# Last row chunk of the last round loaded one strip wide instead of the last two; ScalarE makes most of the last scalings

## The reference

```python
# layer 0: e is x times two small weights
h   = adj @ (adj.T @ e)
out = layernorm(h) * gamma + beta + x
x   = layernorm(x + out)
# layer 1
deg  = adj.sum(axis=0) + 1.0
dinv = rsqrt(deg)
z    = dinv[:, None] * (x @ W)
out  = dinv[:, None] * (adj.T @ z + z) + b
x    = layernorm(x + relu(out))
```

## Time and profile before

| | us |
|---|---|
| median of three runs | 608.97 |
| the profiled execution's own time | 609.2 |
| its span in the trace | 607.4 |
| TensorE matmul busy | 578.3 (95%) |
| VectorE busy | 346.3 (57%) |
| ScalarE busy | 178.5 (29%) |
| GpSimd busy | 115.2 (19%) |

### The profile page before, as it was taken

The page is one execution under the profiler, slowest core; times in us unless marked ns, Lnnn a source line. Parts: engine busy times, 40 slices in busy tenths (PEclk is TensorE's granted clock), DMA queues, the critical chain, the costliest instruction groups (busy, mean ns, idle before and its releaser), DMA issues.

```text
span 607.4 us, 10911 instructions
## 1 busy us (share of the span) xinstructions
PE 578.3 (95%) x4648; PEld 219.9 (36%) x4648; DVE 346.3 (57%) x464; ACT 178.5 (29%) x432; POOL 115.2 (19%) x166
## 2 busy tenths in 40 slices
PE   9979999999999999999999999999999999877794
PEld 6423333333333333333333334544433334222232
DVE  3996676878868676986766694555520004400026
ACT  2035080633618062351807148334000001000001
POOL 3007052250706132050504114101000000000000
PEclk9989999999999999999999999999999999999998
DMA  9999796969788795978889597799999999999992
GB/s 312 386 377 363 249 350 223 389 221 354 269 307 319 260 386 190 384 270 307 287 287 387 187 391 271 293 399 378 422 421 422 421 419 422 420 420 423 412 387 101
DMA packets 77401, 204.82 MB, mean 337 GB/s; under 512 B 4126, under 2 KB 6686, under 8 KB 68136
## 3 DMA queue, kind: packets, MB, share of 16 engines
q1 hardware_dynamic: 76288, 203.27, 88.6%
q10 hardware_dynamic: 1064, 0.84, 0.4%
HBM read 202.79 MB, written 1.31 MB: 336 GB/s over the span
## 4 chain that ended last, share of the span: by engine, by line
PE 79%; DMA 14%; SPq 3%; DVE 2%; ACT 1%; issue 0%; DVEq 0%
PE psum L876 32%; PE psum L969 24%; PE psum L1056 14%; DMA turned<-in_adj_dram 7%; PE psum L977 5%; DMA slot<-in_adj_dram 4%; SPq L308 3%; DMA last_slot<-in_adj_dram 3%; PE psum L1076 1%; PE psum L931 1%; PE psum L1034 1%; PE psum L943 1%; SPq L312 0%; DVE slot L699 0%; DVE C L751 0%
## 5 line engine op out<-in xcount | busy, mean ns | idle before, releaser
L693 DVE STREAM_TRANSPOSE slot<-slot 128x2048 f32<-128x2048 f32 x80 | 178.1, 2281 | 68.4 <-PE psum L876 68.4
L876 PE MATMUL psum<-slot,E 128*64 128x512 f32 x800 | 180.0, 597 | 1.2 <-DMA slot<-in_adj_dram 0.7
L969 PE MATMUL psum<-slot,T 32*64 32x512 f32 x2560 | 144.1, 596 | 3.3 <-DVE T L674 3.3
L1056 PE MATMUL psum<-slot,E 128*64 128x512 f32 x480 | 106.2, 594 | 11.2 <-DMA slot<-in_adj_dram 11.0
L876 PEld LDWEIGHTS psum<-slot,E 128*64 128x64 f32 x800 | 54.4, 137 | 113.0 <-issue 108.8
L422 POOL COPY turned<-last_slot 32x1024 f32<-32x1024 f32 x80 | 84.1, 1052 | 38.9 <-issue 31.2
L969 PEld LDWEIGHTS psum<-slot,T 32*64 32x64 f32 x2560 | 55.9, 133 | 89.5 <-issue 82.1
L483 ACT ACTIVATE turned<-last_slot 32x1024 f32<-32x1024 f32 x80 | 84.3, 1054 | 5.3 <-DVE last_slot L693 3.6
L817 DVE TENSOR_TENSOR T<-psum,dinv 128x256 f32<-128x256 f32 x10 | 4.2, 424 | 134.5 <-PE psum L1076 134.0
L1056 PEld LDWEIGHTS psum<-slot,E 128*64 128x64 f32 x480 | 35.2, 137 | 79.1 <-issue 78.9
L475 ACT ACTIVATE T<-turn 32x186 f32<-32x186 f32 (+4 forms) x200 | 53.5, 309 | 21.2 <-DVE turn L668 19.0
(11 more groups left out here) (112 smaller groups left out, 273.1 us busy)
## 6 DMA issues: line engine op xcount, KB each, us to landing
slot<-in_adj_dram SPq DMA_DIRECT2D x152, 1024.0 KB, 14.2
last_slot<-in_adj_dram SPq DMA_DIRECT2D x30, 1024.0 KB, 7.8
turned<-in_adj_dram SPq DMA_DIRECT2D x9, 1024.0 KB, 16.1
X<-in_x_dram SPq DMA_DIRECT2D x5, 256.0 KB, 4.4
turned<-in_adj_dram SPq DMA_DIRECT2D x2, 512.0 KB, 12.1
out_dram<-T ACTq DMA_DIRECT2D x6, 128.0 KB, 7.0
out_dram<-T SPq DMA_DIRECT2D x4, 128.0 KB, 2.6
beta_b<-in_L_gnn_ln_beta_dram SPq DMA_DIRECT2D x1, 32.0 KB, 11.6
```

What stands on the lines that cost most here:

```text
L693: v.transpose(parts, parts).then_inc(chunk_cut, 1)
L876: return mm(acc[half[b % 2], :], E[:, b, :], view[:, b % CB, :], start=(b < 2), stop=(b >= NB - 2))
L969: last = mm(acc[half[h], a, :], T[step % 2][rows_a, jb, d, :], slot[step % 2][rows_a, h:NF:2, :, cols], start=step == 0 and jb == 0 and d ...
L1056: last = mm(bank[ACC[RES + n // NB * WIDE + s]][half[b % 2], :], E[:, b, :], wide[i % PLACES][:, s * JW:(s + 1) * JW], start=(b < 2), stop ...
```

## The change

`TAIL` becomes 76: loads 72 to 75 are wide, with chunk 8's four row blocks for all four strips, and only chunk 9 is loaded one strip at a time, by loads 76 to 79 (strips 6, 7, 8, 9). A strip turns complete with each of these loads. `turn_o(6)` comes after the sweep of load 77, `turn_o(7)` after that of 78, `turn_o(8)` and `turn_o(9)` after that of 79.

In strips 6, 7 and 8 ScalarE makes all four scalings, in strip 9 the first two. For that VectorE makes `shift = -mean * rstd` (one operation of 128x4, kept in `rsum`, two places), and ScalarE computes `rstd * o + shift` with an Identity activation whose scale and bias are columns in SBUF. `o` and `rstd` have two places in turn, so that strip J waits for the scalings of strip J - 2 only. This holds for all ten strips.

```diff
-TAIL = LOADS - WIDE * 2
+TAIL = LOADS - WIDE
+SCALED = {NJ - 4: 4, NJ - 3: 4, NJ - 2: 4, NJ - 1: 2}
...
+        shift = rsum[:, :].rearrange("p (i b) -> p i b", b=JB)
...
         def tail_part(n):
-            i = n - TAIL
-            return NQ - 2 + i % 2, NJ - WIDE + i // 2
+            return NQ - 1, NJ - WIDE + n - TAIL
...
-                    before_tail = 2 * (NJ - 1 - J) if J >= NJ - WIDE else 0
+                    before_tail = NJ - 1 - J if J >= NJ - WIDE else 0
...
                 nc.scalar.activation(std[:, 0:JB], mean_var[:, :, 1], ACT.Sqrt, bias=eps_col[:, 0:1])\
                   .then_inc(o_root, 1)
+                blocks = SCALED.get(J, 0)
+                if blocks:
+                    act.wait_ge(o_shift, J - NJ + WIDE + 1)
+                    if J >= RES:
+                        act.wait_ge(out_stored[J % RES], J // RES * 16)
+                for jb in range(blocks):
+                    nc.scalar.activation(Y[1][:, J % RES * JB + jb, :], Y[0][:, J % 2 * JB + jb, :], ACT.Identity,
+                                         bias=shift[:, J % 2, jb:jb + 1], scale=rstd[:, J % 2 * JB + jb:J % 2 * JB + jb + 1])\
+                      .then_inc(out_ready, 1)
...
-                o, r = Y[0][:, 0:JB, :], rstd[:, 0:JB]
+                lo = J % 2 * JB
+                o, r = Y[0][:, lo:lo + JB, :], rstd[:, lo:lo + JB]
...
-                if J >= 1:
-                    dve.wait_ge(out_ready, JB * J)
+                if J >= 2:
+                    dve.wait_ge(out_ready, JB * (J - 1))
...
-                for jb in range(JB):
+                ours = SCALED.get(J, 0)
+                if ours:
+                    v.scalar_tensor_tensor(shift[:, J % 2, :], mean_var[:, :, 0], -1.0, r, ALU.mult, ALU.mult)\
+                     .then_inc(o_shift, 1)
+                for jb in range(ours, JB):
...
             for n in range(TAIL, LOADS):
                 tail_sweep(n)
-                if n % 2 == 0 and n > TAIL:
-                    turn_o(NJ - WIDE + (n - TAIL) // 2 - 1)
+                if n > TAIL:
+                    turn_o(NJ - WIDE + n - TAIL - 1)
             turn_o(NJ - 1)
```

More of the change, by code:

```diff
@@ L226, in build @@
         o_root = sem("o_root")
+        o_shift = sem("o_shift")
         out_ready = sem("out_ready")
```

## The result

The changed kernel was slower: 612.23 us median of 13 runs (611.46 to 614.98) against 609.92 of 13 (607.56 to 610.84), ratio 1.0051 with a 95% interval of 1.0035 to 1.0067. The medians are 2.3 us apart, the ratio says 3.1. Four more timings of the same kernel gave 1.0032 (1.0011 to 1.0052), 1.0012 (0.9994 to 1.0030), 1.0043 (1.0024 to 1.0062) and 1.0040 (1.0021 to 1.0058). The mean of the five is 1.0036, 2.2 us. The first was the highest of them. Two executions of all that follow, one of 689.8 us and one of 1550.1, were disturbed and are in no ratio.

A forecast was written before the change was run, and what follows sets the result against it. DMA bounds the kernel from 540 us, VectorE already sets the end by 0.4 us. Loads 0.9 us sooner, but strips queuing on VectorE, give +2.10 us: 609.2 to 611.3, median 0.2 lower, 611.1; range 609.3 to 612.8.

The forecast's parts named there:

- The loads: Loads 72 to 75 at the end of the stream: made wide, they bring all that follows 0.9 us sooner.
- TensorE and the start of strip 6: TensorE's sweeps and turnings at the end: VectorE starts strip 6 at 593.71 us, before at 586.37.
- The queue: Strips 6 to 9 at the end: they queue on VectorE from 593.71 us, one every 3.20 us instead of 4.07.
- The next strip starts at 3.20: VectorE in the last strips: the shift ends 3.16 us after a strip's start, the next strip starts at 3.20.
- the two are level, and I count no wait: Start of strip 8: ScalarE's path takes 6.39 us from strip 6's start, VectorE's two periods 6.40, so no wait.
- ScalarE's scaling: One scaling on ScalarE takes 0.45 us at a pace of 0.35, four take 1.50.
- Rival (b): ScalarE's scalings hold up the copies of strips 8 and 9; 612.5 us at 0.60 each; chance 0.14.
- The split of strip 9's scalings: Last strip, scalings shared by ScalarE and VectorE: ends 4.00 us after its start, against 3.96 with all four on VectorE.
- The sum: End of the kernel: the last scaling moves from 605.21 to 607.31 us, +2.10 us, store and end unchanged.
- About 0.5%, 3 us, is what a measurement of this kernel tells from no change.: Whole kernel's timing: smaller differences count as no change, which got 0.75.
- TensorE's work is no more than it was.: TensorE at the end, sweeps and turnings up to sweep 79's end at 598.4 us: no work added.

The follow-up runs named there:

- Chunk 8 narrow: The changed kernel, but loads 72 to 75 bring chunk 8 one strip at a time; ratio 1.0064 to the kernel before.
- The tail alone: The kernel before with only the change's new load order (TAIL = 76), one place and all scalings on VectorE; ratio 1.0080 to the kernel before.
- scalings twice: The changed kernel with four more ScalarE activations before the scalings of strip 6 and four before those of strip 7; ratio 1.0064 to the kernel before.
- the version that beat both: The changed kernel, but loads 72 to 75 bring chunks 8 and 9 for strips 6 and 7 only; ratios 0.9970 and 0.9981 to the kernel before.

## Why the prediction was right or wrong

The time, 612.23 us, lies within the range, 1.1 above the 611.1 that was said. Of this 0.95 is the kernel before, which took 609.92 in this timing and not 608.97. The direction failed: 0.75 was given to no change that can be told, and the kernel was slower, 1.0051 with an interval clear of 1. Two steps failed; they stand behind those that held.

**The loads.** Right. Said: 0.9 us sooner. Chunk 8 narrow puts it at 0.88 where strip 6 starts and at 0.8 at the end.

**TensorE and the start of strip 6.** Right. Said: 593.71, 18.35 behind the pair; measured 594.49 - 576.21 = 18.28.

**The queue.** The mechanism was right: four strips on VectorE with no time between them, one in 3.2 us where the loads bring one in 2.7. The tail alone shows its cost, 4.7 us; the scalings on ScalarE and the two places take back 2.9 of it, where 2.4 were said. Two sizes were off. "The next strip starts at 3.20": the next strip begins 0.08 after the shift begins, while the shift still runs (597.46, 597.54), so the period is 3.05. And "the two are level, and I count no wait" holds for strip 9 but for strip 8 the path over ScalarE came 0.17 later than VectorE. Strips 6 to 9 took 9.34 instead of 9.60.

**ScalarE's scaling.** Worked out from rows as 0.45 at a pace of 0.35, four in 1.50; measured 0.426 and four in 1.44. The Trainium skill's formula ("ScalarE: Activation LUTs", section "What ACT_TABLE_LOAD costs") gave 0.425 and 1.42, so the trace agrees with the page better than with my rows. Rival (b) was closer to deciding than its 0.14 says: scalings twice shows that four more activations, 1.33 us on ScalarE, are paid in full, and the root behind them as well. The split of strip 9's scalings was said to take 4.00 us for the strip against 3.96 with VectorE alone; it took 3.93 (603.83 to 607.76).

**The sum.** Said: +2.10 for the place of the change; the profile has +1.75 (and 33.8 us from the pair instead of 34.1). The 0.35 less are 0.07 at the start of strip 6, 0.26 in the queue, 0.07 in strip 9, and 0.05 more behind it. Put against the timings, the sum was good: +2.10 is 0.35%, and the mean of the five ratios says 0.36%. Part of that is luck, since a sum 0.35 too high stood in for what the timings have above the place.

**"About 0.5%, 3 us, is what a measurement of this kernel tells from no change."** This step failed, and it turned a right sum into a wrong call. The sum says 0.35% slower, and this sentence made no change of it, with 0.75. No row stood behind it. The interval of the first timing reaches 0.16% to either side, those of the next four 0.18 to 0.21%, and four of the five are clear of 1. A slowdown of 2.1 us can be told, and the call that followed from the sum was slower.

**"TensorE's work is no more than it was."** This step failed too, and it bears on the size: I counted TensorE's work, put its idle time at nothing, and gave no reason. The path over ScalarE to turning 9 leaves TensorE idle for 1.95 us where it was 0.70. In two of six profiles the clock had fallen by the turning, which puts 0.87 us on the path. If that were the share in all executions, it would be 0.3 us (an estimate), and 1.75 + 0.3 = 2.05 stands beside the 2.2 of the five ratios. It doesn't explain the first timing's profile, in which turning 9 took 1.10 us.

**The rest of the first ratio** (3.1 us against 2.2) stays open. Where the mean granted clock of an execution is the highest that its kernel shows (0.997 or more before, 0.996 changed), 24 executions of before, beside the second to fourth timing, average 608.2 us and eight of the changed kernel 609.8: 1.6 us, near the 1.75 of the profile. The first timing of the changed kernel had none at 0.996. What it had is four of 13 at 0.985 to 0.987, which took 613.7 to 615.0 us, where the other nine average 612.0. Over the five timings 14 of 61 executions of the changed kernel have a mean clock of 0.988 or less, and of before, beside the last four, 8 of 109, none of them above 612.2 us. So part of the cost may sit in executions with a lower clock, more than turning 9 alone would take. No profile is of such an execution of the changed kernel, and where its clock fell isn't known.

## What to carry to other kernels

Before loads at the end of a stream are put together, compare the time that finishing one result takes with the time between results. Here 4.06 us of finishing, or 3.1 with ScalarE's help, met a load every 2.7, and 0.9 us of faster loads became a queue that cost 4.7, or 1.75 with the help. Before a small cost is called no change, ask what the interval of a timing is. Put together those results that still have room behind them and leave the last two apart, as in the version that beat both. When a step goes to another engine, walk that engine's whole list behind it, roots and copies too, and look for what new idle time of TensorE stands just ahead of a matmul on the path.

## What the runs showed of the hardware

- The rate of these 1 MB loads rises with the size of the contiguous piece: 387 GB/s at 2 KB, 409 at 4 KB, 419 at 8 KB, each from 576 to 582 us.
- The granted clock falls to half also in the midst of the work. At 42 to 44 us, busy time by stretch of the kernel before, and of the changed kernel's second profile:

```profile
42.00:44.00 2.00, 2.00 (x24) 0.76 (x16) 2.00 (x2) 1.90 (x8) 0.58 (x4) 0.50 1.05 387
```

```profile
42.00:44.00 2.00, 2.00 (x48) 0.96 (x40) 2.00 (x2) 1.90 (x8) 0.72 (x4) 1.00 1.06 388
```

  With the clock at 0.50 TensorE gets through 24 matmul records in 2 us, and 48 without. In twelve of fifteen profiles the clock falls there, and from 50 to 590 us it is 1.00 in all fifteen. From 40 to 42 us TensorE is busy for 0.52 to 1.41 of 2 us in the profiles with the fall and for 0.64 to 1.20 in those without, so its busy time there doesn't tell them apart. The three without have the pair 70/71 at 573.9 us, all others at 574.7 to 576.6, whatever the kernel. Of the kernel before, beside the last four timings of the changed one, 26 executions with a mean clock of 0.997 or more average 608.2 us, and 22 at 0.995 average 609.8. One of its profiles is of each kind, 0.998 without the fall and 0.995 with it. So this is a good part of the spread between executions, and about as large as what the change costs.
- An operation of VectorE that doesn't need the one ahead of it starts 0.08 us after a 128x4 operation began that lasts 0.16.
